# Both FFNs' normalisations on ScalarE, a sixth C product on GpSimd, and a new order of stages, in a fused macaron layer

## The chip, the cores and the metric

One core of one Trainium2 chip. The metric is the device time of one launch in microseconds (us), here the median of three runs.

## The reference

32 sequences of 256 tokens with H = 128 channels, float32. Three parts follow one another on the residual x:

```python
x = x + 0.5 * _L0_ffn_ref(_layernorm(x), Wg, bg, W1, b1, W2, b2)
x = x + _L0_attn_ref(_layernorm(x), norm_w, in_proj_w, conv_w, conv_b, ..., out_proj_w)
x = x + 0.5 * _L0_ffn_ref(_layernorm(x), Wg, bg, W1, b1, W2, b2)
```

The FFN has eight experts of 128 x 128 and takes, for each token, the output of the expert with the largest gate:

```python
logits = xf @ Wg + bg
idx = argmax(softmax(logits))
h = gelu(einsum('th,ehi->tei', xf, W1) + b1)       # exact gelu
y = einsum('tei,eih->teh', h, W2) + b2
out = y[idx]
```

The middle part is a Mamba block with its own residual (D_IN = 256, N = 16 states, convolution of 4 taps):

```python
xn = rmsnorm(x) * norm_w
x_path, z_path = split(xn @ in_proj_w.T)
x_path = silu(causal_conv(x_path) + conv_b)
dt_x, Bm, Cm = split(x_path @ x_proj_w.T)
dt = softplus(dt_x @ dt_proj_w.T + dt_proj_b)
h = exp(dt * A) * h + (dt * x_path) * Bm           # over the 256 tokens
y = sum_n(h * Cm) + D_param * x_path
return (y * silu(z_path)) @ out_proj_w.T + residual
```

## The kernel before

The 8192 tokens are cut into 16 chunks of 512 (two sequences). A software pipeline runs over iterations `i0` from -4 to 16. In one iteration the state recurrence of chunk i0 is made, the first FFN (f1) of chunk i0+3 and its second products for i0+2, the projections x, z, bc, dt of the Mamba block for i0+2 and i0+1, the out projection and the gate of the second FFN (f2) for i0-1, and the products of f2 for i0-1 to i0-3. Every iteration has 16 slots. Nothing schedules by itself: a `Plan` gives for each engine the slot (with .5 or a sub-position 0 to 3) at which a stage stands in that engine's program, and semaphores hold an instruction back until its inputs and its buffer are ready.

What the engines do in a slot s of the recurrence (half a head, one group q of four states, 1024 columns in two halves of 512, "units" 2s and 2s+1):

- GpSimd (`state_bx`, L1112) writes dtx * B into `hb`, two slots ahead.
- ScalarE (`make_decay`, L775) writes exp(A dt) of a half into one of three PSUM banks `dA`, two halves ahead. It waits until the half that last had this bank is read.
- VectorE (`state_unit`, L914) runs the recurrence of a half as a scan and then multiplies by C: scan in L926 and product in L930. For the slots in `POOL_C` (1, 2, 5, 9, 14) the scan writes to `hb` (L924), and GpSimd makes the product of both halves (`product_c`, L1120).
- TensorE (`sum_states`, L606) adds up the states of two slots into the PSUM bank `Y`.

Around it stand the other stages. Two PSUM banks `G` are shared by the transposes, gates and projections, in the order of the plan (`BANK` gives the bank, `g_full` and `g_free` the hand-over). A first product of an expert (`first_product`, L562 with the bias and L563) goes to the bank `PH`; ScalarE copies it out (`take_first`, L731), and the gelu over four experts comes later (`gelus`, L751), between two table loads. Second products (L594) of an FFN gather in the bank `PY`, which VectorE adds to X (L983). A layer norm has its statistics on VectorE (`norm_stats`), the inverse root on GpSimd (`inverse_root`, L1052) and the normalisation (`normalize`, L1079): (x - mean) * rstd, four instructions of 128 columns (L1085). The transposes of the result on TensorE (L542) go to a G bank, which ScalarE copies out (L724), the gate product (L661) and VectorE's one-hot code (L957 to L968) with its transposes (L670) follow.

The out projection (L641) of the plan's stage "out" writes bank 0 of G, after z0 in the same bank has been read by ScalarE's silu (L805). VectorE adds it to X (L983, the second such). The silu of x (L780) is made behind that of z, and needed by the products bc and dt (L550). ScalarE reads the bank of dt twice (L818, L820), then makes the softplus (L824, L826), GpSimd adds (L1140) and multiplies (L1145), and the results go through DRAM to be replicated. All DMAs are issued by SyncE in the order of its own plan.

## Time and profile before

| | us |
|---|---|
| median of 3 runs | 1329.93 |
| lowest and highest | 1327.08, 1342.4 |
| the profiled execution, its own time | 1330.48 |
| its span in the profile | 1328.7 |

The profile shows one execution. Engines are PE (TensorE), PEld (its weight loads), DVE (VectorE), ACT (ScalarE), POOL (GpSimd) and SP (SyncE). An idle time in brackets is that of the engine just before the instruction, and behind the arrow stands what released it. The granted clock is given as a share of 2.4 GHz. Line numbers are those of the kernel before.

### The profile page before, as it was taken

How to read it: one execution, taken by the hardware profiler on the slowest of the kernel's cores; microseconds unless marked ns; L12 is line 12 of the kernel's file. 1: busy time of each engine (PE TensorE's matmuls, PEld its weight loads, DVE VectorE, ACT ScalarE, POOL GpSimd, SP SyncE). 2: the span in 40 equal slices, each digit the busy share in tenths (PEclk: the TensorE clock that was granted, in tenths of full speed). 3: DMA queues.
4: the chain of work that ended last, by engine and by line, in shares of the span. 5: the costliest groups of instructions: out<-in, count | busy, mean ns of one | idle time of the engine just before them, and what ended most of it. 6: DMA issues, size and time to landing. Idle time of an engine off the chain costs nothing.

```text
span 1328.7 us, 16290 instructions
## 1 busy us (share of the span) xinstructions
PE 1142.2 (86%) x5188; PEld 579.9 (44%) x5188; DVE 1060.7 (80%) x1713; ACT 857.7 (65%) x1159; POOL 1067.7 (80%) x900
## 2 busy tenths in 40 slices
PE   6886868799999898999989898998989896969588
PEld 3432324244535444544445454454435443524246
DVE  2317989988898988888988988888888889888930
ACT  2327475777768687767768677767768686574531
...
DMA packets 60405, 130.02 MB, mean 98 GB/s; under 512 B 7744, under 2 KB 26864, under 8 KB 52128
## 3 DMA queue, kind: packets, MB, share of 16 engines
...
q8 instruction: 42, 0.69, 0.2%
...
## 4 chain that ended last, share of the span: by engine, by line
PE 59%; DVE 21%; ACT 8%; issue 6%; POOL 5%; SPq 0%; DMA 0%; DVEq 0%; ACTq 0%; POOLq 0%
PE PY L594 17%; PE PH L563 12%; PE G L550 9%; DVE dA L926 8%; PE Y L606 7%; DVE hb L924 4%; PE PH L562 4%; PE G L641 3%; DVE hb L930 3%; PE G L542 2%; PE dA L576 2%; POOL hb L1112 2%; DVE stat L905 2%; ACT hs L751 1%; ACT dA L775 1%
## 5 line engine op out<-in xcount | busy, mean ns | idle before, releaser
L1112 POOL TENSOR_TENSOR hb<-dtx_rep,bs 128x1024 f32<-128x1024 f32 x256 | 598.7, 2359 | 0.0
L926 DVE TENSOR_TENSOR_SCAN dA<-dA,hb 128x512 f32<-128x512 f32 x352 | 429.1, 1219 | 23.8 <-ACT dA L775 16.8
L775 ACT ACTIVATE dA<-dt_rep,A 128x512 f32<-128x512 f32 x512 | 343.7, 690 | 115.9 <-DVE hb L930 97.6
L594 PE MATMUL PY<-W,hs 128*128 128x128 f32 x2048 | 298.6, 289 | 0.0
L594 PEld LDWEIGHTS PY<-W,hs 128*128 128x128 f32 x2048 | 261.9, 196 | 82.8 <-issue 72.1
L731 ACT COPY hs<-PH 128x512 f32<-128x512 f32 x232 | 135.2, 583 | 237.7 <-PE PH L563 235.0
L563 PE MATMUL PH<-xnT,W 128*128 128x512 f32 x464 | 280.5, 688 | 0.0
L930 DVE TENSOR_TENSOR hb<-dA,cs 128x512 f32<-128x512 f32 x352 | 243.5, 692 | 24.8 <-DVE dA L926 0.5
L1120 POOL TENSOR_TENSOR hb<-hb,cs 128x1024 f32<-128x1024 f32 x80 | 188.7, 2359 | 85.0 <-DVE hb L924 85.0
L924 DVE TENSOR_TENSOR_SCAN hb<-dA,hb 128x512 f32<-128x512 f32 x160 | 186.4, 1206 | 8.9 <-ACT dA L775 6.8
L606 PE MATMUL Y<-hb,Sel 128*32 128x512 f32 x1024 | 161.3, 707 | 29.5 <-POOL hb L1120 19.6
L562 PE MATMUL PH<-ohT,Lm 24*128 24x512 bf16 x232 | 93.8, 404 | 44.9 <-ACT hs L731 42.8
L751 ACT ACTIVATE hs<-hs 128x2048 f32<-128x2048 f32 x58 | 110.5, 1912 | 0.3
L563 PEld LDWEIGHTS PH<-xnT,W 128*128 128x128 f32 x464 | 72.7, 197 | 57.0 <-issue 57.0
L943 DVE SCALAR_TENSOR_TENSOR xs<-G,Wc,xs 128x506 f32<-128x506 f32 (+2 forms) x96 | 67.5, 739 | 37.6 <-ACT xs L795 34.8
L562 PEld LDWEIGHTS PH<-ohT,Lm 24*128 24x128 bf16 x232 | 21.2, 91 | 146.7 <-ACT hs L731 82.6
L641 PE MATMUL G<-Wo,y 128*128 128x128 f32 x256 | 49.4, 373 | 32.3 <-ACT zs L805 32.3
L1057 POOL TENSOR_SCALAR neg<-mv 128x4 f32<-128x4 f32 x48 | 9.7, 201 | 81.9 <-DVE mv L911 81.9
L606 PEld LDWEIGHTS Y<-hb,Sel 128*32 128x32 f32 x1024 | 21.6, 115 | 109.6 <-issue 73.4
L1140 POOL TENSOR_TENSOR dt<-dt,sp 128x1024 f32<-128x1024 f32 x16 | 37.8, 2364 | 38.3 <-ACT sp L826 38.3
L641 PEld LDWEIGHTS G<-Wo,y 128*128 128x128 f32 x256 | 46.4, 280 | 45.2 <-issue 44.9
L957 DVE TENSOR_TENSOR G<-G,Bg 128x32 f32<-128x32 f32 x32 | 6.1, 190 | 73.4 <-PE G L661 73.4
...
## 6 DMA issues: line engine op xcount, KB each, us to landing
...
```

Of the source, the lines that this page charges most:

```text
L562: nc.tensor.matmul(PH[:, :], Lm[:, e, :], ohT[:, w, (it.i0 + off) % 2, :], start=True, stop=False)
L563: nc.tensor.matmul(PH[:, :], W1[:, e, :], xnT[:, w, :], start=False, stop=True).then_inc(ph_full, 1)
L594: last = nc.tensor.matmul(PY[:, P * j:P * (j + 1)], hs[:, w, e, P * j:P * (j + 1)], W2[:, e, :], start=False, stop=e == E - 1 and j == J - 1)
L606: last = nc.tensor.matmul(Y[D32 * g:D32 * (g + 1), :], Sel[:, :], hb[:, (2 * k + g // 2) % HR, g % 2], start=k == 0, stop=q == NQ - 1)
L641: last = nc.tensor.matmul(G[b][:, P * j:P * (j + 1)], y2[:, h, P * j:P * (j + 1)], Wo[:, h, :], start=h == 0, stop=h == HF - 1)
L731: nc.scalar.copy(hs[:, w, e, :], PH[:, :]).then_inc(ph_free, 1)
L775: nc.scalar.activation(dA[u % NA][:, :], dt_rep[:, h, g, :], ACT.Exp, scale=A[:, h, g, q:q + 1]).then_inc(decay, 1)
L924: nc.vector.tensor_tensor_scan(x_in_hb, a, x_in_hb, 0.0, ALU.mult, ALU.add).then_inc(scan, 1)
L926: nc.vector.tensor_tensor_scan(a, a, x_in_hb, 0.0, ALU.mult, ALU.add).then_inc(scan, 1)
L930: nc.vector.tensor_tensor(x_in_hb, a, cs[:, q, :], ALU.mult).then_inc(prod, 1)
L1112: nc.gpsimd.tensor_tensor(hb[:, s % HR], dtx_rep[:, h, 2 * m:2 * m + 2, :], bs[:, q, None, :].broadcast_to([P, 2, CH]), ALU.mult).then_inc ...
L1120: nc.gpsimd.tensor_tensor(hb[:, s % HR], hb[:, s % HR], cs[:, q, None, :].broadcast_to([P, 2, CH]), ALU.mult).then_inc(prod_p, 1)
```

## The change

Seven edits go together:

1. "out" no longer uses a G bank. It writes `Y`, the bank of the state sums, which is idle between two chunks, and stands one and a half slots earlier. The first sum of the next chunk waits until VectorE has read it (`out_read`).
2. Both `normalize` go from GpSimd to ScalarE, as four activations x * rstd + shift each, where GpSimd makes the new value shift = -mean * rstd (one small instruction more). f2's stands behind slot 7, f1's behind slot 14.
3. Slot 12 joins `POOL_C`: its product goes from VectorE to GpSimd.
4. Expert 4 of f1 in the steady iterations uses the bank `PY` instead of `PH`. It waits for VectorE's addition of f1 (`y_added`), and the second products of f2 wait for its copy.
5. First products of f1 (experts 4 to 7) and of all of f2 stand earlier, by up to a slot; the transposes oh_f1 stand in slot 5 instead of 6; on ScalarE dt0 comes half a slot later.
6. Decay 2 of the next chunk is made at the end of iteration slot 15 and decay 14 in slot 5, ahead of dt0 (`EARLY`); GpSimd makes the input of slot 5 right behind that of slot 4 (`EARLY_B`). ScalarE makes the silu of x ahead of that of z.
7. VectorE has new places between the two halves of a slot: f1's one-hot code at 1.25 instead of 1.0, the addition of "out" at 3.25 instead of behind that of f2 at 3.5.

The core of the diff:

```diff
-BANK = {"ln_f1": 0, "z0": 0, "out": 0, "bc": 0, ...
+BANK = {"ln_f1": 0, "z0": 0, "bc": 0, ..., "out": None}
 STEADY = Plan(
-    stages=[..., ("out", 3, 1), ("bc", 4, 1), ("dt1", 5, 0), ("dt0", 5, 1), ("oh_f1", 6, 0), ...
+    stages=[..., ("out", 2, 2), ("bc", 4, 1), ("dt1", 5, 0), ("dt0", 5, 1), ("oh_f1", 5, 1), ...
...
-    dve={"gate_f1": 1.0, "gated1": 1.5, "y_f2": [(3.5, -3)], "out": 3.5, ...
+    dve={"gate_f1": 1.25, "gated1": 1.5, "y_f2": [(3.5, -3)], "out": 3.25, ...
+IN_PY = (0, 4)
+EARLY = {(15, 0): 2, (5, 1): 14}
+EARLY_B = {2: 5}
-POOL_C = (1, 2, 5, 9, 14)
+POOL_C = (1, 2, 5, 9, 12, 14)
```

```diff
 def first_product(it, w, e, off):
-    it.wait_unit(pe, ph_free, w, e, 0)
-    nc.tensor.matmul(PH[:, :], Lm[:, e, :], ohT[...], start=True, stop=False)
-    nc.tensor.matmul(PH[:, :], W1[:, e, :], xnT[:, w, :], start=False, stop=True).then_inc(ph_full, 1)
+    if in_py(it.plan, w, e):
+        it.wait(pe, y_added[0], off - 1, 1, 1)
+        bank, full = PY, py_full
+    else:
+        it.wait_unit(pe, ph_free, w, e, 0)
+        bank, full = PH, ph_full
+    nc.tensor.matmul(bank[:, :], Lm[:, e, :], ohT[...], start=True, stop=False)
+    nc.tensor.matmul(bank[:, :], W1[:, e, :], xnT[:, w, :], start=False, stop=True).then_inc(full, 1)
 def sum_states(it, off, k):
     if k == 0:
-        it.wait(pe, gated, off, HF, 0)
+        it.wait(pe, out_read, off - 1, 1, 1)
 # "out" on TensorE
-    it.wait_free(pe, g_free, "out")
-            last = nc.tensor.matmul(G[b][:, P * j:P * (j + 1)], y2[...], Wo[:, h, :], ...)
-    last.then_inc(g_full[b], 1)
+            last = nc.tensor.matmul(Y[:, P * j:P * (j + 1)], y2[...], Wo[:, h, :], ...)
+    last.then_inc(out_made, 1)
 # ScalarE
+def normalize(it, w, off):
+    it.wait(act, rooted[w], off, 1, 1)
+    if it.has(off - 1):
+        Iteration(...).wait_read(act, g_free, f"ln_f{w + 1}")
+    for j in range(J):
+        last = nc.scalar.activation(xn[:, w, j, :], X[...], ACT.Identity,
+                                    scale=rstd[:, w, j:j + 1], bias=shift[:, w, j:j + 1])
+    last.then_inc(normed[w], 1)
 # ScalarE, the end of a slot
-    stages(it, s + 0.5)
+    for k in range(2):
+        if k:
+            stages(it, s + 0.5)
+        if (s, k) in EARLY and it.has(off):
+            make_decay(it, off, EARLY[s, k])
 # GpSimd, inverse_root for the two FFNs
+    nc.gpsimd.tensor_tensor(shift[:, w, :], neg[:, w, :], rstd[:, w, :], ALU.mult).then_inc(rooted[w], 1)
-def normalize(it, w, off):
-    ...
-        last = nc.gpsimd.tensor_scalar(xn[...], X[...], neg[...], rstd[...], ALU.add, ALU.mult)
```

In the rows below a name in brackets is the semaphore on which the instruction waits; "x3" in a row of its own stands for three of the kind above, without a wait.

TensorE around "out", before. L594 is the last second product of f2, L562 and L563 the first products, L606 a state sum, L641 "out":

```order
L594 MATMUL PY<-W,hs 128x128 [waits gelu_f2]
L594 MATMUL PY<-W,hs 128x128 x3
L562 MATMUL PH<-ohT,Lm 128x512 [waits ph_free]
L563 MATMUL PH<-xnT,W 128x512
L641 MATMUL G<-Wo,y 128x128 [waits g0_free,gated]
L641 MATMUL G<-Wo,y 128x128 x7
L606 MATMUL Y<-hb,Sel 32x512 [waits prod_p,prod,gated]
L606 MATMUL Y<-hb,Sel 32x512 x3
L562 MATMUL PH<-ohT,Lm 128x512 [waits ph_free]
L563 MATMUL PH<-xnT,W 128x512
```

The same place now (L617, L583 and L584, L629, L662):

```order
L583 MATMUL PH<-ohT,Lm 128x512 [waits ph_free]
L584 MATMUL PH<-xnT,W 128x512
L617 MATMUL PY<-W,hs 128x128 [waits gelu_f2]
L617 MATMUL PY<-W,hs 128x128 x3
L662 MATMUL Y<-Wo,y 128x128 [waits gated]
L662 MATMUL Y<-Wo,y 128x128 x7
L583 MATMUL PH<-ohT,Lm 128x512 [waits ph_free]
L584 MATMUL PH<-xnT,W 128x512
L629 MATMUL Y<-hb,Sel 32x512 [waits prod_p,prod,out_read]
L629 MATMUL Y<-hb,Sel 32x512 x3
```

"out" lost its wait for bank 0, and stands ahead of a first product instead of behind it. The first sum, which was behind "out" directly, now waits for VectorE to read it.

TensorE around the products bc and dt (L550), before, from the second half of dt on. The transposes oh_f1 are L670:

```order
L606 MATMUL Y<-hb,Sel 32x512 [waits prod_p,prod]
L606 MATMUL Y<-hb,Sel 32x512 x3
L592 MATMUL PY<-b_part,ohT 128x128 [waits gelu_f1,y_added_f2]
L594 MATMUL PY<-W,hs 128x128
L592 MATMUL PY<-b_part,ohT 128x128
L594 MATMUL PY<-W,hs 128x128
L592 MATMUL PY<-b_part,ohT 128x128
L594 MATMUL PY<-W,hs 128x128
L592 MATMUL PY<-b_part,ohT 128x128
L594 MATMUL PY<-W,hs 128x128
L670 MATMUL G<-Idb,oh 24x128 [waits g1_free,gate_f1]
L670 MATMUL G<-Idb,oh 24x128 x3
```

Now (L566 for the projections, L691 for oh_f1):

```order
L583 MATMUL PH<-ohT,Lm 128x512 [waits ph_free]
L584 MATMUL PH<-xnT,W 128x512
L566 MATMUL G<-xs,Wxdt 128x512 [waits g1_free]
L566 MATMUL G<-xs,Wxdt 128x512
L566 MATMUL G<-xs,Wxdt 128x512 [waits g0_free]
L566 MATMUL G<-xs,Wxdt 128x512
L691 MATMUL G<-Idb,oh 24x128 [waits g1_free,gate_f1]
L691 MATMUL G<-Idb,oh 24x128 x3
L629 MATMUL Y<-hb,Sel 32x512 [waits prod_p,prod]
L629 MATMUL Y<-hb,Sel 32x512 x3
```

oh_f1 moved from behind the sum and the first second product to directly behind dt0. It waits for bank 1, which dt1 had.

ScalarE between the taps of the convolution (L795) and the decays of the next chunk, before. L731 are copies of PH, L775 decays:

```order
L795 ACTIVATE xs<-G,Bc,Wc 128x512 [waits g1_full,summed]
L795 ACTIVATE xs<-G,Bc,Wc 128x512 [waits g0_full]
L731 COPY hs<-PH 128x512 [waits ph_full,w2_done_f1]
L775 ACTIVATE dA<-dt_rep,A 128x512 [waits prod]
L775 ACTIVATE dA<-dt_rep,A 128x512 [waits scan]
L731 COPY hs<-PH 128x512 [waits ph_full,w2_done_f2] x2
L775 ACTIVATE dA<-dt_rep,A 128x512 [waits prod,dt0_in]
```

Now (L836 taps, L766 copies, L812 decays, L753 the normalisations of f1):

```order
L836 ACTIVATE xs<-G,Bc,Wc 128x512 [waits g1_full,summed]
L836 ACTIVATE xs<-G,Bc,Wc 128x512 [waits g0_full]
L766 COPY hs<-PH 128x512 [waits ph_full,w2_done_f2]
L812 ACTIVATE dA<-dt_rep,A 128x512 [waits prod]
L812 ACTIVATE dA<-dt_rep,A 128x512 [waits scan]
L753 ACTIVATE xn<-X,shift,rstd 128x128 [waits g0_free,rooted_f1]
L753 ACTIVATE xn<-X,shift,rstd 128x128 x3
L766 COPY hs<-PH 128x512 [waits ph_full,w2_done_f2]
L812 ACTIVATE dA<-dt_rep,A 128x512 [waits prod,dt0_in]
```

The four normalisations stand between the decays of slot 15 and a copy of PH; the copies are those of one expert later.

## Rows read from the trace of the kernel before

**Rows 1.** Page of the profile, part 1: busy us, share of the span, instructions

```profile
PE 1142.2 (86%) x5188; PEld 579.9 (44%) x5188; DVE 1060.7 (80%) x1713; ACT 857.7 (65%) x1159; POOL 1067.7 (80%) x900
```

**Rows 2.** Chain of work that ended last: start us, us, what

```profile
412.54 3.44 PE G L641 x16
...
1013.04 3.56 PE G L641 x16
```

**Rows 3.** Timeline of TensorE, 700 to 790 us: start us, us, instruction, [idle before <-releaser]

```profile
712.74 3.53 PE L641 MATMUL G<-Wo,y 128*128 128x128 f32 x16 [2.14 <-ACT zs L805]
...
723.59 1.88 PE L550 MATMUL G<-xs,Wxdt 128*128 128x512 f32 x4
...
749.10 0.39 PE L562 MATMUL PH<-ohT,Lm 24*128 24x512 bf16 x1 [2.73 <-ACT hs L731]
...
755.94 0.66 PE L542 MATMUL G<-Id,xr 128*128 128x128 f32 x4 [1.23 <-POOL xr L1095]
...
761.71 1.98 PE L550 MATMUL G<-xrT,Win 128*128 128x512 f32 x4 [0.45 <-ACT xrT L724]
...
777.49 0.95 PE L661 MATMUL G<-Wg,xnT 128*128 128x8 f32 x8
...
786.93 3.17 PE L641 MATMUL G<-Wo,y 128*128 128x128 f32 x16 [2.14 <-ACT zs L805]
```

**Rows 4.** Timeline of VectorE, 700 to 790 us and after 1095

```profile
718.37 1.20 DVE L926 TENSOR_TENSOR_SCAN dA<-dA,hb 128x512 f32<-128x512 f32 x1
...
742.00 0.69 DVE L983 SCALAR_TENSOR_TENSOR X<-PY,X 128x512 f32<-128x512 f32 x1 [1.09 <-PE PY L594]
...
780.10 2.34 DVE L924 TENSOR_TENSOR_SCAN hb<-dA,hb 128x512 f32<-128x512 f32 x2 [0.21 <-DVE oh L968]
...
1173.62 1.23 DVE L926 TENSOR_TENSOR_SCAN dA<-dA,hb 128x512 f32<-128x512 f32 x1 [1.86 <-ACT dA L775]
```

**Rows 5.** Windows: busy us of PE, PEld, DVE, ACT, POOL; granted clock; DMA share; GB/s

```profile
262.00:265.00 3.00, 1.24 (x11) 1.17 (x11) 2.90 (x4) 2.99 (x4) 3.00 (x2) 1.00 0.00 0
712.00:715.00 3.00, 2.27 (x11) 2.30 (x11) 2.86 (x5) 2.98 (x4) 3.00 (x2) 0.58 0.00 0
826.00:829.00 3.00, 2.67 (x11) 0.95 (x6) 2.93 (x12) 2.23 (x4) 3.00 (x4) 0.50 0.01 3
```

**Rows 6.** Timeline of TensorE in three other stretches

```profile
263.86 2.02 PE L641 MATMUL G<-Wo,y 128*128 128x128 f32 x16 [1.76 <-ACT zs L805]
...
837.76 1.88 PE L550 MATMUL G<-xrT,Win 128*128 128x512 f32 x4
...
1291.49 0.26 PE L592 MATMUL PY<-b_part,ohT 24*128 24x128 bf16 x1 [0.85 <-ACT hs L751]
```

**Rows 7.** Groups of 562.5 to 862.5 us: count, busy us, mean ns, idle before

```profile
L926 DVE TENSOR_TENSOR_SCAN dA<-dA,hb 128x512 f32<-128x512 f32 x88 | 107.3, 1219 | 4.4 <-ACT dA L775 2.3 <-DVE oh L968 1.2 <-DVE xs L943 0.9
...
L563 PE MATMUL PH<-xnT,W 128*128 128x512 f32 x128 | 76.6, 681 | 0.0
...
L930 DVE TENSOR_TENSOR hb<-dA,cs 128x512 f32<-128x512 f32 x89 | 61.6, 692 | 6.2
L1120 POOL TENSOR_TENSOR hb<-hb,cs 128x1024 f32<-128x1024 f32 x20 | 47.2, 2359 | 15.4 <-DVE hb L924 15.4
...
L751 ACT ACTIVATE hs<-hs 128x2048 f32<-128x2048 f32 x16 | 30.6, 1914 | 0.1
...
L1085 POOL TENSOR_SCALAR xn<-X,neg,rstd 128x128 f32<-128x128 f32 x32 | 14.0, 452 | 0.8
...
L795 ACT ACTIVATE xs<-G,Bc,Wc 128x512 f32<-128x512 f32 x8 | 6.2, 778 | 7.8 <-PE G L550 7.7
...
L780 ACT ACTIVATE xs<-xs 128x1024 f32<-128x1024 f32 x4 | 4.2, 1058 | 0.0
```

**Rows 8.** Timeline of ScalarE, 700 to 790 us

```profile
724.59 0.68 ACT L820 ACTIVATE sp<-G,Bdt 128x512 f32<-128x512 f32 x1
...
777.66 1.28 ACT L757 ACT_TABLE_LOAD   x1
```

More of the change, by code:

```diff
@@ L46 @@
 LN_OFF = {0: 3, 1: -1}
-BANK = {"ln_f1": 0, "z0": 0, "out": 0, "bc": 0, "dt0": 0, "gate_f2": 0, "ln_p": 0, "x0": 0,
-        "gate_f1": 1, "z1": 1, "dt1": 1, "oh_f1": 1, "ln_f2": 1, "oh_f2": 1, "x1": 1}
+BANK = {"ln_f1": 0, "z0": 0, "bc": 0, "dt0": 0, "gate_f2": 0, "ln_p": 0, "x0": 0,
+        "gate_f1": 1, "z1": 1, "dt1": 1, "oh_f1": 1, "ln_f2": 1, "oh_f2": 1, "x1": 1, "out": None}
 OFF = {"ln_f1": 3, "gate_f1": 3, "oh_f1": 3, "ln_p": 2, "x1": 2, "x0": 2, "z0": 1, "z1": 1, "bc": 1, "dt1": 1, "dt0": 1,
@@ L183, in g_uses, with in_py, count @@
     return n + sum(BANK[use] == BANK[name] and has(i, OFF[use]) for use in seq[:seq.index(name)])
+def in_py(plan, w, e):
+    return plan is STEADY and (w, e) == IN_PY
 def w1_uses(i, w, e):
-    n = sum(has(k, off) for k in range(FIRST, i) for *_, off in plan_of(k).w1_order)
+    def count(k, order):
+        return sum(has(k, off) and not in_py(plan_of(k), v, u) for *_, v, u, off in order)
     order = plan_of(i).w1_order
     at = [unit[2:4] for unit in order].index((w, e))
-    return n + sum(has(i, off) for *_, off in order[:at])
+    return sum(count(k, plan_of(k).w1_order) for k in range(FIRST, i)) + count(i, order[:at])
 def direct_no(w, chunk, e):
@@ L747, in gelus @@
                     it.wait_unit(act, ph_free, w, E - 1, 1)
+                    if w == 0 and it.plan is STEADY:
+                        it.wait(act, py_free, 0, 1, 1)
                 for k in range(2):
@@ L787, in stages @@
                         copy_out(it, f"ln_f{w + 1}", xnT[:, w, :])
+                if t == at.get("norm_f2") and it.has(-1):
+                    normalize(it, 1, -1)
+                if t == at.get("norm_f1") and it.has(4):
+                    normalize(it, 0, 4)
                 if t == at.get("ln_p") and it.has(2):
@@ L848, in body @@
                     take_units(it, s, 0)
-                    if it.has(off):
+                    if it.has(off) and 2 * t not in EARLY.values():
                         make_decay(it, off, 2 * t)
@@ L1020, in stages @@
                 if t == at.get("stats_f2") and it.has(-1):
[L1021 removed]
+                    it.wait(dve, out_read, -1, 1, 1)
                     norm_stats(it, 1, -1)
@@ L1127, in stages @@
                     inverse_root(it, 1, -1)
-                if t == at.get("norm_f2") and it.has(-1):
-                    normalize(it, 1, -1)
                 if t == at.get("root_p") and it.has(2):
```

94 lines of the change are left out of this document (47 added, 47 removed).

## The prediction

> **What bounds the kernel now.** I read the shares of the engines first, then the groups of a stretch of four periods, the chain, the timelines of each engine over one period, and last the granted clock. No engine is full: TensorE 86%, VectorE and GpSimd 80%, ScalarE 65% of the span [rows 1]. So the time is set by a loop of waits. In the chain the out projection returns every 75.06 us on average (1013.04 - 412.54 over eight periods) [rows 2]. Periods come in two kinds. I lay a short one out between three marks [rows 3, 4]: VectorE adds the first FFN to X at 742.00; 19.7 us later TensorE starts the x products (761.71); and 54.5 us after those (25.2 to the out projection at 786.93, then, by the period before, 29.3 from 712.74 to 742.00) comes the next addition, right behind the last second product. That is 74.2 us.
>
> In it TensorE waits four times, 6.6 us in all [rows 3]: 2.14 before the out projection, until ScalarE has read z0 out of the bank that "out" needs; 2.73 before a first product, because the copy of PH stands behind a table load and the first gelu; and two short ones. The wait before "out" costs more than itself. Its granted clock is 0.58 in 712 to 715 [rows 5], the level of 1.2 GHz for most of it, and the sixteen passes of "out" take 3.53 us there, where the same sixteen took 2.02 us at 263.86, with the clock at 1.00 [rows 5, 6]. I count 1.5 us for such a fall. In the long kind of period the fall behind the gelu lasts longer (0.50 at 826 to 829) [rows 5], and the x products start 21.5 us after the addition (837.76, the addition being at 786.93 + 29.3) instead of 19.7 [rows 3, 6].
>
> **First addition to x products: 0 to -0.4 us.** The product of slot 12 leaves VectorE: two instructions of 0.69 us; a slot with them takes 3.8 us, one without 2.3, so 1.5 [rows 4, 7]. They lie between the addition and the decay that holds up xrT, so xrT is ready earlier; only the 0.45 us wait before the x products can go. Expert 4 of the first FFN now goes to PY and fills the 2.73 us wait with 1.4 us of product and a sum. But the next unit still waits for a copy behind the second gelu, and the transposes of xr still hang on VectorE's statistics and GpSimd's root and normalisation, and come 14 us after the addition (755.94, behind 1.23 us of wait for GpSimd) [rows 3, 4]: that chain is untouched. The wait moves behind it. I take 0, and the same mixture of short and long.
>
> **X products to VectorE's second recurrence of slot 1: -0.5 us.** Before, gate_f1 ends 16.7 us after the x products (777.49 + 0.95) and the second recurrence of slot 1 starts at +19.5 (half of the pair at 780.10) [rows 3, 4]. Now one first-product unit less lies in between (64 units cost 76.6 us in their L563 part, so 1.2, and about 1.4 with L562) [rows 7]. Against that, ScalarE has four normalisations to do between the decays of slot 15 and the copy for which TensorE's next unit waits. No row shows such an instruction. By size, two SBUF rows (L780, 1058 ns for 1024 elements, and L751, 1914 for 2048) give 0.83 ns an element; from the 778 ns of L795, which also has scale and bias as operands, 384 elements fewer leave 0.46 us, and four overlapping ones some 1.5 us. Bounds: 1.2 us below, four times 778 ns, 3.1 us, above [rows 7]. (The Trainium skill, page "ScalarE: Activation LUTs", section on the cost of an ACTIVATE, gives 186 ns + 0.833 ns per element + 93 ns per pointer operand, 93 ns of it overlapped: 1.64 us for four, which would add 0.1 us a period.) With 1.5 us the copy ends 7.55 us after the x products, where TensorE wanted it at 6.7: a wait of 0.8 us. gate_f1 then ends at 16.3. But ScalarE is later too: its second table load, which ended at 778.94 (+17.2) [rows 8], ends at +18.3, and the decay of the second half at +19.0. Since the first recurrence now stands ahead of the gating, VectorE goes on at +19.0 instead of +19.5.
>
> **To the second addition: -1.4 us with the half above.** VectorE from +19.0: rest of slot 1 and y2 1.7, slot 2 2.25, half of slot 3 1.9, X+out 0.7, other half 1.9, X+PY 0.6, statistics 1.3: slot 4 starts at +29.4, before at +30.85 (718.37 is 5.63 behind its "out") [rows 4]. VectorE's wait for "out" and TensorE's 2.14 are gone. Slot 4 takes 3.8, the first recurrence of slot 5 1.2: +34.4. Behind that ScalarE makes one decay (0.7) and reads dt1 twice (1.25, the second in 0.68 [rows 8]): +36.35. TensorE is faster: from gate_f1's end at 16.3 through z, two units, two w2, "out" at full clock (2.0), a unit, the sum, bc, a unit, dt1 and dt0 I count 18.1 us, so +34.4. And here is the new wait. The transposes oh_f1 now stand directly behind dt0 and need the bank of dt1, which ScalarE lets go at +36.35. Before they came behind a sum and 2.3 us of second products. Queued behind them are the sum of slots 2 and 3 and everything of the first FFN. From there 16.6 us of TensorE work lead to the second addition, as before (725.4 to 742.0) [rows 3, 4]: +53.0 instead of +54.5. Of TensorE's 3.6 us at "out", 1.95 come back as this wait. VectorE, done with slot 9 before, idles.
>
> **The clock takes part of it: +0.9 us.** A wait of 1.95 us is near to the 2.14 us after which the clock fell. Bounds: 0 and 1.5 us; I take a fall in six of ten periods. The Trainium skill speaks against this term: its page "TensorE: Matmul & The Clock Gate", section "Part 1: The HAM clock gate", has the ramp at under 1% of a typical kernel span and advises against fitting it. Here 1.5 us of 75 are 2% for each fall. By that rule both the old 1.5 and the new 0.9 drop out, nothing is left of the gain in a period, and the sum would be 1322; the measured passes decide, so I keep the term.
>
> **Other edits: nothing.** The GpSimd balance is two normalisations (2 x 1.75 with overlap) out, one product of 2.36 and two small ones of 0.27 in [rows 7]; the sixth product ends about 5.2 us behind the x products, 0.5 before its sum is wanted. The early recurrence input, C2 right behind C1 and x_silu first move work inside ScalarE's and GpSimd's idle time. norm_f2 fits where ScalarE waited for PH. SP's c2 now waits for the GpSimd product, some 0.6 us later, with more than 20 us in hand.
>
> **Ends: -8 us.** The last four chunks have no first FFN ahead of them or little; VectorE is nearly full. There the 1.5 us count in full, four times: -6.0. The decay pulled ahead of dt0 takes away a wait of VectorE in slot 7, 1.86 us at 1173.62 [rows 4] and some 1.7 in the period before: -3.5. At the very end ScalarE normalises behind both gelus. Before, the transposes ran during them, and second products began at 1291.49, 0.85 behind [rows 6]; now 1.5 us of normalisation, the transposes and their latency come on top, 3.8, less one unit and copy of 2.2 that was done earlier: +1.6.
>
> **Sum.** A period: 0 - 1.4 + 0.9 - 0.1 (short waits) = -0.6. Twelve periods: -7. With the ends -15. The profiled execution took 1330.48 us by its own clock (span 1328.7), so 1315.5; the median of three is 0.55 lower: 1315.
>
> **Rivals.** First, the clock does not fall at oh_f1, and with fuller stretches the long kind of period vanishes too: -1.5 and the 0.9 between a short period and the mean, twelve times, and -8 at the ends: 1293. For it: the wait of 1.76 us before "out" at 263.86 left the clock full [rows 5, 6]. Against it: the second gap behind the gelu stays. 0.30.
>
> Second, the fall comes in each period: -1.4 + 1.5 a period comes to +1 in twelve, with the ends 1323, no change that can be told. 0.20.
>
> Third, slower: ScalarE's normalisations cost what L795 costs. The chain from the x products through ScalarE's gelus grows by 1.6 us a period, and TensorE's wait for PH reaches 2.4 us, long enough for a fall as well as that at oh_f1. -1.4 + 1.5 + 1.6 = +1.7, times twelve, less 8: 1342. It decides from about 2.6 us for the four. For it: copies and decays queue behind them. Against it: the sizes. 0.12. My forecast has 0.38.
>
> **Range.** The main case with its bounds goes from 1305 to 1326; the rivals stretch it to 1291 and 1338. A measurement of this kernel can tell about 1% from no change, 13 us. Faster by over 1% (below 1316.6): rival one and half of the main case, 0.50. Slower: 0.12. Same: 0.38.
>
> **What would show it.** Right: "out" without a wait and at full clock; a wait of about 2 us at oh_f1 on ScalarE's read of dt1; VectorE waiting 1 to 3 us for the second products before the addition; four normalisations in 1.5 us; VectorE's wait at slot 7 gone; a mean period near 74.4. Wrong: no wait at oh_f1 (the gain is then 2 us and more), normalisations of 0.6 us and longer, or a new wait of VectorE for bx or of TensorE for the GpSimd product of slot 12.

## The result

| | us |
|---|---|
| predicted | 1315.0 (1291 to 1338) |
| changed kernel, median of 4 runs | 1356.07 (1347.27 to 1359.36) |
| kernel before, measured beside it, median of 4 | 1328.51 |
| ratio, 95% interval | 1.0157 (1.0110 to 1.0204) |
| profiled execution of the changed kernel, its own time and span | 1354.01, 1352.2 |

The change made the kernel 1.6% slower, outside the range and on the other side. (The ratios here and below leave aside an execution that took over 1.5% longer than the fastest one of its kernel.) Read in the two traces, the 23.5 us between the spans (1328.7 and 1352.2) lie like this:

| stretch, by its first x product | before | changed | difference |
|---|---|---|---|
| start to the first x product after 300 us | 311.63 | 326.92 | +15.3 |
| ten periods from there | 749.80 | 764.64 | +14.8 |
| from there to the end | 267.3 | 260.6 | -6.6 |

The ends came out near the forecast of -8. The ten periods went from a mean of 74.98 to 76.46 us, where 74.4 was forecast, and the start had no term in the sum at all.

The page of the changed kernel, part 1 and the row of the granted clock in forty slices, against [rows 1]:

```profile
PE 1150.1 (85%) x5188; PEld 572.5 (42%) x5188; DVE 1036.9 (77%) x1681; ACT 899.5 (67%) x1287; POOL 1055.0 (78%) x820
...
PEclk9888969897989999898979989797999988878689
```

VectorE and GpSimd have less to do than before, ScalarE 42 us more. TensorE, with the same 5188 instructions, is busy 8 us longer: its instructions take longer, there are not more of them.

**The fill.** ScalarE's timeline over the first 30 us. The first fence is the changed kernel, the second the kernel before; the number in brackets is the idle time ahead:

```profile
25.41 1.65 ACT L753 ACTIVATE xn<-X,shift,rstd 128x128 f32<-128x128 f32 x4 [14.89 <-POOL shift L1108]
27.07 1.28 ACT L777 ACT_TABLE_LOAD   x1
28.36 0.60 ACT L777 ACTIVATE hs<-PH 128x512 f32<-128x512 f32 x1
```

```profile
10.34 1.28 ACT L742 ACT_TABLE_LOAD   x1
17.70 0.60 ACT L742 ACTIVATE hs<-PH 128x512 f32<-128x512 f32 x1 [6.08 <-PE PH L576]
```

ScalarE works in order. In the fill's plan the normalisation of chunk 1 stands ahead of the direct gelus of chunk 0, and its data come late; so it waits 14.89 us, and the first gelu starts at 28.36 instead of 17.70. On GpSimd nothing was queued behind that wait.

**A steady period.** TensorE's timeline of the changed kernel from an addition of f1 (VectorE's row, 761.54) to the x products (L566, 784.52) and on to oh_f1 (L691), against [rows 3, 4]:

```profile
761.54 0.69 DVE L1025 SCALAR_TENSOR_TENSOR X<-PY,X 128x512 f32<-128x512 f32 x1 [1.26 <-PE PY L617]
```

```profile
768.64 0.38 PE L583 MATMUL PH<-ohT,Lm 24*128 24x512 bf16 x1 [0.36 <-ACT hs L766]
768.96 1.13 PE L584 MATMUL PH<-xnT,W 128*128 128x512 f32 x2
770.01 0.39 PE L691 MATMUL G<-Idb,oh 128*24 128x128 bf16 x4
772.84 0.60 PE L583 MATMUL PH<-ohT,Lm 24*128 24x512 bf16 x1 [2.43 <-ACT hs L766]
773.37 2.07 PE L584 MATMUL PH<-xnT,W 128*128 128x512 f32 x2
775.45 1.11 PE L558 MATMUL G<-Id,xr 128*128 128x128 f32 x4
...
784.52 3.62 PE L566 MATMUL G<-xrT,Win 128*128 128x512 f32 x4
...
809.76 1.95 PE L662 MATMUL Y<-Wo,y 128*128 128x128 f32 x16
...
819.79 1.98 PE L566 MATMUL G<-xs,Wxdt 128*128 128x512 f32 x4 [0.92 <-ACT bcT L745]
823.55 0.38 PE L691 MATMUL G<-Idb,oh 128*24 128x128 bf16 x4 [1.78 <-ACT sp L858]
```

Much is as forecast. "Out" (L662) has no wait and takes 1.95 us instead of 3.17 to 3.56 [rows 2, 3]. The new wait at oh_f1 stands where it was put, on the softplus's read of the dt1 bank, with 1.78 us for 1.95. But between the addition and the x products, where the forecast had 0 to -0.4 us, there are 23.0 us, and every pass behind the wait of 2.43 us takes double: L584 has 2.07 us for what took 1.13 just ahead. The windows of the changed kernel show why (busy us of PE, PEld, DVE, ACT, POOL; granted clock; DMA share; GB/s):

```profile
769.00:772.00 3.00, 1.41 (x7) 0.47 (x6) 2.86 (x4) 2.98 (x3) 2.68 (x8) 1.00 0.01 3
772.00:775.00 3.00, 2.16 (x3) 0.60 (x3) 2.97 (x12) 1.98 (x4) 3.00 (x5) 0.57 0.00 0
775.00:778.00 3.00, 3.00 (x7) 1.31 (x7) 2.70 (x4) 1.79 (x3) 2.90 (x6) 0.50 0.46 175
...
784.00:787.00 3.00, 3.00 (x5) 1.53 (x6) 0.00 (x0) 0.47 (x1) 3.00 (x2) 0.50 0.25 87
787.00:790.00 3.00, 3.00 (x6) 0.80 (x5) 1.76 (x3) 1.08 (x2) 3.00 (x2) 0.59 0.77 213
790.00:793.00 3.00, 3.00 (x20) 1.39 (x18) 2.48 (x4) 2.76 (x6) 3.00 (x3) 1.00 0.57 229
...
820.00:823.00 3.00, 1.77 (x4) 0.47 (x3) 3.00 (x4) 2.16 (x4) 1.75 (x2) 1.00 0.09 22
823.00:826.00 3.00, 2.45 (x19) 1.24 (x19) 2.86 (x4) 2.97 (x5) 2.12 (x1) 1.00 0.02 5
```

The clock falls to the level of 1.2 GHz behind that gap and stays there for some 17 us, though TensorE is busy all through, and the x products still run in it (3.62 us for the 1.88 to 1.98 of [rows 3, 6]). At the wait of oh_f1 (820 to 826) it does not fall at all. In the kernel before, the low stretch behind the gelu was some 3.5 us in one period and 10 in the next, here in its windows:

```profile
750.00:753.00 3.00, 3.00 (x14) 0.70 (x12) 2.86 (x4) 2.97 (x4) 2.84 (x6) 0.50 0.01 3
753.00:756.00 3.00, 1.77 (x6) 0.46 (x5) 2.86 (x12) 2.13 (x4) 2.90 (x6) 0.93 0.08 29
...
825.00:828.00 3.00, 2.67 (x14) 0.97 (x7) 2.97 (x7) 2.97 (x5) 2.92 (x5) 0.52 0.01 3
...
834.00:837.00 3.00, 3.00 (x16) 1.02 (x11) 2.95 (x4) 2.27 (x4) 2.82 (x7) 0.77 0.00 0
```

In the changed kernel it is 7 to 17 us in each period (read in windows of 0.5 us). VectorE and ScalarE then wait for the x products. The fence shows two groups of the changed kernel over 590 to 890 us, four periods; the last numbers are the idle time before them. In the kernel before the same two groups waited 2.0 us (taps on VectorE) and 7.8 us (L795) in such a stretch:

```profile
L985 DVE SCALAR_TENSOR_TENSOR xs<-G,Wc,xs 128x506 f32<-128x506 f32 (+2 forms) x24 | 17.1, 742 | 19.3 <-ACT xs L836 18.7
...
L836 ACT ACTIVATE xs<-G,Bc,Wc 128x512 f32<-128x512 f32 x8 | 6.2, 777 | 20.9 <-PE G L566 20.9
```

So addition to x products went from a mean of 20.5 to 22.4 us, and x products to addition from 54.5 to 54.05. The second was forecast as 53.0 (without the clock term): it is 52.9 in four of ten periods, and 53.8 to 55.4 in the other six, in which the x products themselves ran wholly or partly at the low clock.

### The profile page after: what moved, and what is told of

It is laid out like the page before. It is cut to its first block, busy times and chain, and to the rows that moved or that the text cites. A ratio compares the mean times of both kernels' runs of the same rounds, so it can differ in the third digit from the quotient of the medians.

```text
span 1352.2 us, 16303 instructions
## 1 busy us (share of the span) xinstructions
PE 1150.1 (85%) x5188; PEld 572.5 (42%) x5188; DVE 1036.9 (77%) x1681; ACT 899.5 (67%) x1287; POOL 1055.0 (78%) x820
## 4 chain that ended last, share of the span: by engine, by line
PE 45%; ACT 19%; DVE 19%; issue 11%; POOL 4%; SPq 1%; DMA 0%; DVEq 0%; ACTq 0%; POOLq 0%
PE PY L617 15%; PE PH L584 10%; DVE dA L968 8%; ACT hs L788 5%; PE Y L629 5%; ACT dA L812 4%; PE G L566 4%; DVE hb L966 3%; PE PH L583 3%; DVE hb L972 3%; ACT hs L766 2%; ACT L794 2%; PE G L558 2%; PE PY L615 2%; DVE X L1025 2%
## 5 line engine op out<-in xcount | busy, mean ns | idle before, releaser
L968 DVE TENSOR_TENSOR_SCAN dA<-dA,hb 128x512 f32<-128x512 f32 x320 | 390.3, 1220 | 15.3 <-ACT dA L812 9.0
L812 ACT ACTIVATE dA<-dt_rep,A 128x512 f32<-128x512 f32 x512 | 339.5, 688 | 66.7 <-DVE hb L972 49.7
L617 PE MATMUL PY<-W,hs 128*128 128x128 f32 x2048 | 303.6, 293 | 0.0
L617 PEld LDWEIGHTS PY<-W,hs 128*128 128x128 f32 x2048 | 266.6, 199 | 85.7 <-issue 74.9
L1153 POOL TENSOR_TENSOR hb<-hb,cs 128x1024 f32<-128x1024 f32 x96 | 226.3, 2358 | 88.4 <-DVE hb L966 88.4
L766 ACT COPY hs<-PH 128x512 f32<-128x512 f32 x219 | 127.6, 583 | 232.5 <-PE PH L584 204.1
L584 PE MATMUL PH<-xnT,W 128*128 128x512 f32 x438 | 274.5, 711 | 0.0
L966 DVE TENSOR_TENSOR_SCAN hb<-dA,hb 128x512 f32<-128x512 f32 x192 | 224.6, 1205 | 27.1 <-ACT dA L812 24.9
L972 DVE TENSOR_TENSOR hb<-dA,cs 128x512 f32<-128x512 f32 x320 | 221.2, 691 | 22.6 <-DVE dA L968 0.5
L629 PE MATMUL Y<-hb,Sel 128*32 128x512 f32 x1024 | 156.3, 684 | 30.3 <-POOL hb L1153 22.8
L583 PE MATMUL PH<-ohT,Lm 24*128 24x512 bf16 x219 | 91.5, 418 | 50.2 <-ACT hs L766 48.1
L584 PEld LDWEIGHTS PH<-xnT,W 128*128 128x128 f32 x438 | 71.8, 206 | 56.7 <-issue 56.7
L583 PEld LDWEIGHTS PH<-ohT,Lm 24*128 24x128 bf16 x219 | 20.1, 92 | 151.7 <-ACT hs L766 109.0
L566 PE MATMUL G<-xs,Wxdt 128*128 128x512 f32 x128 | 62.6, 615 | 13.1 <-ACT bcT L745 13.1
L629 PEld LDWEIGHTS Y<-hb,Sel 128*32 128x32 f32 x1024 | 21.8, 113 | 111.1 <-issue 55.8
L753 ACT ACTIVATE xn<-X,shift,rstd 128x128 f32<-128x128 f32 x128 | 52.4, 481 | 20.7 <-POOL shift L1108 20.7
```

The costliest lines, as they stand in the source:

```text
L583: nc.tensor.matmul(bank[:, :], Lm[:, e, :], ohT[:, w, (it.i0 + off) % 2, :], start=True, stop=False)
L584: nc.tensor.matmul(bank[:, :], W1[:, e, :], xnT[:, w, :], start=False, stop=True).then_inc(full, 1)
L617: last = nc.tensor.matmul(PY[:, P * j:P * (j + 1)], hs[:, w, e, P * j:P * (j + 1)], W2[:, e, :], start=False, stop=e == E - 1 and j == J - 1)
L629: last = nc.tensor.matmul(Y[D32 * g:D32 * (g + 1), :], Sel[:, :], hb[:, (2 * k + g // 2) % HR, g % 2], start=k == 0, stop=q == NQ - 1)
L766: nc.scalar.copy(hs[:, w, e, :], PH[:, :]).then_inc(ph_free, 1)
L812: nc.scalar.activation(dA[u % NA][:, :], dt_rep[:, h, g, :], ACT.Exp, scale=A[:, h, g, q:q + 1]).then_inc(decay, 1)
```

## The experiments

For each trace I add up the windows of 1.5 us between 300 and 1125 us in which the granted clock is under 0.75 ("low"), and take the mean of ten periods from the first x product after 300 us. "y to x" is the time from the addition of f1 to the x products in most of these periods. The executions of one kernel scatter by about 1% around their median, so a difference of a few us between medians is none. The kernel before was measured again beside each group of runs, with medians from 1327 to 1335 us; the ratios are to those, and they are the safer comparison between groups (e1 to e4; e5 to e8; e9 to e12; e13 to e16). Periods, low time and "y to x" are each read from one traced execution.

| kernel | median us (runs) | ratio to before, 95% | period | low | y to x |
|---|---|---|---|---|---|
| before | 1328.51 (4) | | 74.98 | 111 | 19.7 / 21.4 |
| changed | 1356.07 (4) | 1.0157 (1.0110-1.0204) | 76.46 | 138 | 21.7 to 23.0 |
| e1 fill order | 1344.0 (4) | 1.0103 (1.0032-1.0175) | 75.74 | 132 | 21.6 to 23.0 |
| e2 first products of before | 1340.35 (10) | 1.0036 (0.9993-1.0078) | 73.59 | 65 | 19.1 / 21.3 |
| e3 norms on GpSimd | 1327.58 (10) | 0.9962 (0.9928-0.9996) | 75.05 | 134 | 22.0 / 23.0 |
| e4 slot 12 on VectorE | 1356.36 (4) | 1.0172 (1.0094-1.0250) | 76.16 | 143 | 21.7 to 23.0 |
| e5 filler in the gap (on e1) | 1308.98 (4) | 0.9852 (0.9799-0.9905) | 73.22 | 47 | 19.08 |
| e6 = e2 + norms on GpSimd | 1333.84 (10) | 1.0071 (1.0030-1.0112) | 75.16 | 77 | 19.1 |
| e7 = e2 + fill order | 1331.02 (10) | 1.0028 (0.9989-1.0067) | 73.91 | 81 | 19.08 |
| e8 before + "out" in Y | 1341.01 (10) | 1.0093 (1.0064-1.0123) | 75.88 | 116 | 19.7 / 21.5 |
| e9 before + filler | 1338.84 (10) | 1.0079 (1.0054-1.0104) | 75.20 | 81 | 20.7 |
| e10 filler of one product | 1345.49 (4) | 1.0101 (1.0043-1.0159) | 75.85 | 108 | 21.7 to 23.0 |
| e11 f1's rows of before | 1341.40 (10) | 1.0078 (1.0037-1.0119) | 75.41 | 68 | 19.1 / 21.4 |
| e12 f2's rows of before | 1334.89 (10) | 1.0041 (1.0010-1.0071) | 75.17 | 126 | 21.6 / 23.0 |
| e13 filler elsewhere | 1352.11 (4) | 1.0132 (1.0038-1.0226) | 75.32 | 48 | 19.60 |
| e14 = e5 + norms on GpSimd | 1308.91 (4) | 0.9842 (0.9785-0.9898) | 73.76 | 45 | 19.1 |
| e15 changed + filler | 1316.30 (10) | 0.9919 (0.9873-0.9965) | 72.56 | 32 | 19.05 |
| e16 = e5 + slot 12 on VectorE | 1322.01 (10) | 0.9918 (0.9883-0.9953) | 73.69 | 38 | 19.72 |

### The fill: e1

```diff
 FILL[-3]
-    act={"ln_f1": 0, "norm_f1": 1}
+    act={"ln_f1": 0, "norm_f1": 9.5}
```

> The changed kernel, with one number changed: in the fill (iteration -3) ScalarE makes f1's normalisation of chunk 1 at slot 9.5, behind the eight direct gelus of chunk 0, instead of at slot 1 ahead of them. Theory F (the fill): in the changed kernel this normalisation waits 14.9 us for data ahead of the gelus, and that alone moved the first x products from 95.25 to 105.9 us. Then the first x products come back to about 96 and the time is 1356 - 10 = 1346 us. Rival: the delay has another cause or is absorbed before the first steady period (the transposes of chunk 1 now come late): first x products stay at 103 or later, time 1353 to 1358.

1344.0 us, 12 less than the changed kernel (ratio 1.0103 for 1.0157). The first x products start at 94.45, and those of the first period after 300 us at 313.0 instead of 326.9. ScalarE's timeline of e1: the first gelu is back at 17.83, and the four normalisations take the same time without a wait.

```profile
17.83 0.60 ACT L777 ACTIVATE hs<-PH 128x512 f32<-128x512 f32 x1 [6.09 <-PE PH L597]
...
34.97 1.64 ACT L753 ACTIVATE xn<-X,shift,rstd 128x128 f32<-128x128 f32 x4
```

Theory F holds. One number in the plan was some 12 of the 28 us between the medians.

### Undoing one edit: e2, e3, e4

e2 takes the rows of first products and copies from the kernel before and sets `IN_PY = None`, with the two waits for `py_free` out. e3 gives GpSimd both `normalize` at their old places. e4 is one number:

```diff
-POOL_C = (1, 2, 5, 9, 12, 14)
+POOL_C = (1, 2, 5, 9, 14)
```

> The changed kernel, with the places of all first products and of their copies as before, and expert 4 of f1 in PH instead of PY (edits 4 and 5 undone except for oh_f1 and dt0; all else as changed). Theory W (the steady periods grew from 74.98 to 76.46 us because the new places leave a wait of 2.4 us behind the second gelu of f2, after which TensorE's clock stays at its low level up to the x products): the clock is back up before the x products, these start about 20 us after the addition of f1 instead of 22 to 23, and twelve periods give 12 x 1.5 = 18 us: 1338 us. Rival N (ScalarE's normalisations or its other extra work lengthen the period): the period stays near 76.4, time 1352 to 1358.

> The changed kernel, with all normalisations of both FFNs back on GpSimd at their places of before (edit 2 undone, all else as changed). Theories F and W together: the fill is as before (first x products near 96), the steady periods stay near 76.4: 1346 us. Rival N (the normalisations on ScalarE are what lengthens the periods): fill and periods both come back, 1356 - 10 - 18 = 1328 us or less. Against both: GpSimd, with six products and the normalisations, becomes the bound: over 1350.

> The changed kernel, with the product of slot 12 back on VectorE (edit 3 undone, all else as changed). Theories F and W: the period keeps its length to 0.5 us, since neither the gap behind the gelu nor the clock hangs on it, and the ends lose 1.5 us in each of some four chunks: 1356 to 1364 us. Rival P (the sixth product holds up GpSimd's inputs and so VectorE, or TensorE's sum): periods near 75, 1338 to 1345 us.

e2 came to 1340.35: theory W, with periods of 73.59 (expected about 75) and half the low time. Ten such periods are 29 us shorter than in the changed kernel and the time is only 16 us less: in the traced execution the start took 6.7 us longer (333.7 to the first x products after 300 us) and the last stretch 8.0 us (268.7 instead of 260.6), where the first products of before come back too. But e3 came to 1327.58, as rival N had it, 16 us under e1, and kept both its low time (134) and its long way to the x products (22 to 23 us). So W and N each seemed to explain the whole of the steady loss. Part of e3 can be read: x products to "out" take 22.1 us in its shorter periods and 22.9 in those of e1, since the wait of 0.71 us for the copy behind the normalisations (0.8 in the prediction) is gone. The periods of the two profiled executions differ by 0.7 us (75.74 and 75.05), 8 of the 16 us. The other 8 are in no trace: the profiled execution of e1 (1335.77) is the fastest of its four and lies 8.2 us under their median, that of e3 (1327.71) lies at its own. e4 changed nothing, as W expected.

### The clock itself: e5, and its control e13

Both add work that nothing uses to the kernel of e1. It has the same three products into an idle G bank in each steady iteration; e5 puts them ahead of the gap, e13 in slot 9, where TensorE runs without a wait.

```diff
+FILLER = (11, 3)
+if s == FILLER[0] and it.plan is STEADY and it.has(3) and it.has(-1):
+    it.wait_read(pe, g_free, "ln_f2")
+    for _ in range(FILLER[1]):
+        nc.tensor.matmul(G[1][:, :], Win[:, 0:P], W1[:, 0:4, :].rearrange("p e t -> p (e t)"), start=True, stop=True)
```

> The kernel of e1_fill_order (1344.0 us), with work added that nothing uses: in slot 11 of each steady iteration TensorE makes three products of 128 x 512 (about 1.9 us) into bank 1 of G, which is idle there, directly ahead of the first product for which it waits 2.43 us behind the second gelu of f2. Theory C (it is the low clock behind this gap, not the place of the products, that costs the steady periods): the wait shrinks to about 0.5, the clock stays up, the x products start about 20 us after the addition of f1 instead of 21.6 to 23, the periods of 78 us vanish: mean 74.3 instead of 76.2, time 1344 - 12 x 1.8 = 1322 us. Rival D (the gap's delay by itself and the ScalarE work set the period, and the clock is a by-product): added work can't help, 1342 to 1350 us.

> Control of e5_filler: the same three unused products of 128 x 512, but in slot 9, where TensorE runs without a wait of 0.3 us or more, and not in the gap behind the gelu of f2. Theory C (the gain of e5_filler came from filling that gap): here the products cost what they take, 2.84 us in each of 12 periods, and the low clock behind the gelu stays: 1344 + 34 = 1378 us (1360 to 1385). Rival (any added work of TensorE keeps its clock up, wherever it stands): 1305 to 1330 us.

e5: 1308.98 us, 35 less than e1 (by the ratios, 0.9852 for 1.0103, 33) and below the kernel before by 1.5% (0.9799 to 0.9905). TensorE's timeline in e5, and its windows:

```profile
748.44 2.84 PE L730 MATMUL G<-W,Win 128*128 128x512 f32 x6
...
753.39 0.39 PE L584 MATMUL PH<-ohT,Lm 24*128 24x512 bf16 x1 [0.41 <-ACT hs L772]
753.70 1.12 PE L585 MATMUL PH<-xnT,W 128*128 128x512 f32 x2
755.69 0.66 PE L559 MATMUL G<-Id,xr 128*128 128x128 f32 x4 [0.86 <-POOL xr L1134]
...
760.85 1.88 PE L567 MATMUL G<-xrT,Win 128*128 128x512 f32 x4
```

```profile
751.00:754.00 3.00, 2.59 (x10) 0.99 (x10) 2.93 (x11) 2.65 (x5) 2.92 (x5) 1.00 0.01 3
...
757.00:760.00 3.00, 3.00 (x18) 1.07 (x16) 2.86 (x4) 2.19 (x4) 3.00 (x5) 1.00 0.17 57
```

With 2.84 us of idle work the wait of 2.43 shrinks to 0.41, the clock stays at 2.4 GHz, and the x products come 19.08 us after the addition. Eight of the ten periods lack any fall there. In the last five of them the period is 71.99 us, 3 us under that of the kernel before. That is the change and the added products together, against a kernel whose clock still falls; what the change alone is worth with the clock up on both sides, no run shows.

e13 was to cost 34 us and cost 8 by the medians (1352.11, from 1338.93 to 1362.7); without the execution of 1362.7, as in the ratio, the median is 1345.37, and nothing is left that can be told from scatter. Its rows show the same gap, but a short fall:

```profile
773.61 0.38 PE L584 MATMUL PH<-ohT,Lm 24*128 24x512 bf16 x1 [2.43 <-ACT hs L772]
```

```profile
772.00:775.00 3.00, 1.39 (x3) 0.53 (x3) 2.93 (x12) 2.75 (x4) 3.00 (x4) 0.84 0.01 3
775.00:778.00 3.00, 2.70 (x8) 1.11 (x7) 3.00 (x4) 1.79 (x3) 2.90 (x7) 0.59 0.56 153
778.00:781.00 3.00, 3.00 (x17) 1.02 (x15) 2.86 (x4) 2.13 (x4) 2.92 (x5) 1.00 0.08 27
```

The x products follow at 781.91, 19.60 us after the addition. In the first period after 300 us the same kernel has the same gap, but a fall of 17 us, and its x products come 22.99 us after the addition (which is at 306.13):

```profile
317.43 0.60 PE L584 MATMUL PH<-ohT,Lm 24*128 24x512 bf16 x1 [2.43 <-ACT hs L772]
...
329.12 3.62 PE L567 MATMUL G<-xrT,Win 128*128 128x512 f32 x4
```

```profile
318.00:321.00 3.00, 2.99 (x7) 1.17 (x6) 2.97 (x9) 1.45 (x3) 2.90 (x8) 0.50 0.33 79
...
330.00:333.00 3.00, 3.00 (x5) 0.75 (x3) 0.74 (x1) 1.00 (x2) 3.00 (x3) 0.50 0.48 113
```

So with one program and one length of gap the long fall costs 3.4 us, and the gap with its short fall 0.5 (19.60 against the 19.08 of e5): the low clock is the cost, as theory C has it. The periods of e13 without a long fall are 75.1 us, 3.1 above the 71.99 of e5: 2.6 between x products and addition (55.5 for 52.9), where the added products stand, and 0.5 between addition and x products. The low time is 48 us, as in e5. So the rival is partly right too: work put elsewhere shortened the fall, though not the gap, and what that gave back about paid for the work. Each fall here stands behind a wait; how long the low level then lasts hangs on something else as well, which no run here isolates.

### How much filler, and on which kernel: e10, e9, e15

e10 is e5 with `FILLER = (11, 1)`. e9 puts the three products into the kernel before, at the start of slot 11. e15 puts them into the changed kernel, with its fill as it is.

> The kernel of e5_filler with one unused product of 0.95 us instead of three (2.84 us). TensorE's wait behind the gelu is then about 1.5 us instead of 2.43 (without) or 0.41 (with three). Theory: what counts is how much of the stretch TensorE idles, so the clock falls in some periods and for shorter: time between 1344 (none) and 1309 (three), about 1325 us. Rival (any wait of this place drops the clock, the three products helped since they closed it): as without, 1338 to 1346 us. Second rival (a wait of 1.5 us is as harmless as that of 1.78 us at oh_f1): 1305 to 1312 us.

> The kernel before, with the same unused work as in e5_filler: in slot 11 of each steady iteration TensorE makes three products of 128 x 512 (0.95 us each) ahead of the first product that waits 2.73 us behind the second gelu of f2. Theory C (in this kernel, too, it is the low clock behind that gap that costs, 3 us in one period and 9 in the next): no low clock there, the x products 19.1 to 19.7 us after each addition of f1, periods of 75.0 - 1.4 = 73.6 us, time 1330 - 17 = 1313 us (1306 to 1320). Rival (the kernel before has balanced this gap: the wait for GpSimd's xr behind it stays, so that the added work only takes its place): 1325 to 1333 us.

> The changed kernel with the three unused products in slot 11 and nothing else, the fill as changed. Two costs that add up: 1356.1 - 35 (gap behind the gelu) = 1321 us, with periods of 72 and first x products near 106. Rival (the later start shifts periods and clock against each other, so that falls stay in most periods): over 1330 us.

e10: 1345.49, as without; one product leaves a wait of 1.81 us, then one of 1.18 for xr, and the clock falls in each period. e9: my expectation was wrong, 1338.84 instead of 1313. TensorE's timeline of e9:

```profile
764.53 0.39 PE L563 MATMUL PH<-ohT,Lm 24*128 24x512 bf16 x1 [1.07 <-ACT hs L737]
...
767.66 0.66 PE L543 MATMUL G<-Id,xr 128*128 128x128 f32 x4 [1.69 <-POOL xr L1101]
...
768.56 2.08 PE L564 MATMUL PH<-xnT,W 128*128 128x512 f32 x2
...
774.45 1.88 PE L551 MATMUL G<-xrT,Win 128*128 128x512 f32 x4
```

The gap of 2.73 us is closed, but in its place stand a wait for the next copy (1.07) and one for xr (1.69), close together, and behind them the clock falls (L564 at 2.08). The added products only took the place of waits, and the time rose although the low time fell from 111 to 81 us: the sum of low time by itself is not the price, it counts what then ends last. e15: 1316.3, 40 under the changed kernel, the two costs adding up as expected (1321). It beats the kernel before by 0.8% (0.9873 to 0.9965), and all but two of its ten periods are 71.97 us. With the same filler the fill's order is then worth 1316.3 - 1309.0 = 7 us by the medians, for 12 without it.

### The parts with less low clock: e14, e16

> The kernel of e5_filler with both FFNs' normalisations on GpSimd as before. Sizes the normalisations on ScalarE while the clock is held up. My figure of the prediction: a wait of 0.8 us at a copy, so x to out 22.1 instead of 22.87 and periods of 71.2 instead of 71.98: 1309 - 9 = 1300 us. Rival (GpSimd, with six products and the normalisations, now ends last in some waits, as in e6_w1_before_norms_gpsimd): periods of 72.5 or more, 1315 us or more. Second rival (what made e3_norms_gpsimd 16 us faster than e1_fill_order was only the clock's pattern): 1307 to 1311 us.

> The kernel of e5_filler with the product of slot 12 back on VectorE (edit 3 undone). In the steady periods my prediction gave this edit 0 to 0.4 us, since the chain from the addition over the statistics to xr is untouched, and 1.5 us in each of the last four chunks: 1309 + 6 = 1315 us. Rival (with the clock up VectorE is what ends last between the addition and the x products): 1.5 us a period more, 1309 + 24 = 1333 us. Second rival (nothing, as e4_slot12_dve against the changed kernel): 1307 to 1311 us.

e14: 1308.91, equal to e5, and its fill has GpSimd's normalisation as e3's. So once the gap is filled it makes no difference to the time which engine normalises: the 0.71 us at the copy are gone, but the state sum of TensorE waits 1.51 us for GpSimd's product instead, as in e6, where GpSimd has six products and the normalisations:

```profile
763.31 1.63 PE L630 MATMUL Y<-hb,Sel 128*32 128x512 f32 x8 [1.51 <-POOL hb L1156]
```

The second rival had the right time, 1307 to 1311 us, but its reason (the clock's pattern alone) isn't shown: one wait was exchanged for another. e16: 1322.01, 13 us over e5. The x products have a wait of 0.5 us again and come at 19.72 instead of 19.08; undisturbed periods are 72.73 instead of 71.99. The sixth product brings 0.7 us a period, half of the 1.5 that VectorE is spared.

### Putting parts together: e6, e7, e11, e12

e6 is e2 with the normalisations on GpSimd, e7 is e2 with the fill of e1. e11 and e12 split edit 5 on the kernel of e1: e11 has f1's rows (and expert 4) of before, e12 f2's.

> The changed kernel with the first products, PY and both FFNs' normalisations as before (edits 2, 4 and most of 5 undone, so that edits 1, 3, 6, 7 and oh_f1, dt0 stay). Theory of independent costs (fill 11 us; new places of first products 1.5 us a period through the clock; normalisations on ScalarE 0.8 us a period through the copy that they hold up, as x to out was 22.09 in e3_norms_gpsimd and 22.86 in e1_fill_order): periods of 73.4 - 0.8 = 72.6 us, time 1340 - 11 - 10 = 1319 us. Rival: each of the two edits alone already frees the period, and VectorE is the bound then: periods of 73.4 as in e2_w1_of_before, 1329 us.

> The kernel of e2_w1_of_before (1340 us) with the fill's normalisation behind the direct gelus, as in e1_fill_order. Additive: 1340 - 11 = 1329 us, first x products near 95, periods unchanged at 73.4. Rival: the earlier start only shifts the clock's pattern against the periods, and these get longer: 1335 to 1345 us.

> The kernel of e1_fill_order (1344.0 us) with f1's first products and their copies at the places of before and expert 4 in PH, f2's as changed. Theory: it is f1's rows with expert 4 in PY that bring TensorE to the copy behind the second gelu with nothing left to wait for at xr, so the gap leads into a fall in each period; with f1's rows of before it is as e7_w1_before_fill: 1331 us, periods of 74. Rival (it is f2's rows, which crowd the stretch from 14 on): 1340 to 1346 us.

> The kernel of e1_fill_order (1344.0 us) with f2's first products and their copies at the places of before, f1's and expert 4 in PY as changed. The counterpart of e11_f1_rows_before. Theory (f1's rows are the cause): 1340 to 1346 us, falls of 9 to 17 us behind the gelu in each period. Rival (f2's rows): 1331 us.

e7 came to 1331.02, as the additive theory had it. e6 came to 1333.84, not 1319: neither theory, since its sums wait up to 1.50 us for GpSimd. e12 went against its theory: 1334.89, nearer to the rival's 1331 and below e1 with nearly the same low time (126), as x products to "out" take 21.0 to 22.7 us. e11 (1341.40, not 1331) has little low time (68), yet its x products to "out" take 25.1 us: f1's last unit now stands behind the x products together with all of f2's, and TensorE meets three waits on copies there (0.82, 0.71, 0.39). In this pair of runs the rows of f1 decide how long the clock is low, those of f2 how crowded the stretch behind the x products is. The two tables belong together.

### "Out" alone: e8

The kernel before with edit 1 and the place 3.25 on VectorE.

> The kernel before, with edit 1 alone: the out projection goes to the bank Y, one and a half slots earlier, and VectorE adds it at 3.25. My step on this edit: its wait of 2.14 us and the low clock behind it (1.5 us) go, and as oh_f1 stays behind the sum, no wait takes their place except one of VectorE: -1.4 to -2.0 us a period, 12 to 15 periods: 1331 - 20 = 1311 us (1305 to 1318). Rival (the earlier place gains nothing, as the wait was covered by work of ScalarE and VectorE that ends last): 1327 to 1334 us.

1341.01, 0.9% slower instead of 1.4% faster. TensorE's timeline of e8 around the first sum (L608) behind "out":

```profile
791.81 1.06 PE L608 MATMUL Y<-hb,Sel 128*32 128x512 f32 x8 [1.26 <-DVE X L983]
794.15 0.39 PE L564 MATMUL PH<-ohT,Lm 24*128 24x512 bf16 x1 [1.27 <-ACT hs L731]
```

"Out" starts 21.5 us after the x products instead of 25, but the addition of f1 comes no earlier (53.3 to 56.3 us after them, mostly 54.8 and more, instead of 54.5). The wait of 2.14 us is replaced by two of 1.26 and 1.27, because the first sum must now wait until VectorE has read `Y`. In the changed kernel the first products moved earlier cover this.

## Why the prediction was wrong

**The step that failed most** is "First addition to x products: 0 to -0.4 us", with its "I take 0, and the same mixture of short and long". It measured +1.9 us a period (20.5 to 22.4). The step followed the waits rightly, even to "the next unit still waits for a copy behind the second gelu", and the wait shrank from 2.73 to 2.43 and 0.36. What it took as given was the clock behind the wait. In the short periods of the kernel before, TensorE reached the transposes of xr early and idled there for 1.23 us, so a short fall cost little. Expert 4 in PY and the earlier first products changed that: e11, with f1's rows of before, has the waits of 2.73 and 1.21 us again and its x products 19.1 or 21.4 us after the addition. With passes at double length for 7 to 17 us TensorE became what ends last up to the x products. e5 shows the size: with the clock up, the same stretch takes 19.08 us.

**"Other edits: nothing"** failed in the fill. The prediction said that norm_f2 fits into ScalarE's waits and looked at no normalisation ahead of the steady periods. The start cost 11.9 us up to the transposes of chunk 1 (36.57 against 48.47), and e1 gave back 12. The rule that would have caught it stands in the case itself: name what is queued behind a new wait.

**"The clock takes part of it: +0.9 us"** put the fall in the wrong place. The wait at oh_f1 was there (1.78 for 1.95), and the clock stayed at 1.00 there: each of the periods from 300 us on has one low stretch, and it lies behind the gelu. The wait before "out" of 2.14 us had dropped it in the kernel before, so the step went by length alone. But e13 has low stretches of unlike length behind equal waits of 2.43 us (3.5 us, and 17 in its first period after 300 us), so the length of one wait does not decide.

The Trainium skill, page "TensorE: Matmul & The Clock Gate", section "Part 1: The HAM clock gate", has the ramp, the slow first stretch of a kernel's matmuls, at under 1% of a typical kernel span. That figure does not carry over to falls that come back in each period: here the clock is low for 138 of 825 us, and filling one gap was worth 35 us. The prediction set it aside and was right to, yet kept far too little for the clock.

**Right steps.** X products to the second addition: forecast 53.0 against 54.5, measured 52.9 wherever the low clock doesn't reach it; "out" without a wait and at full clock; no wait of VectorE left at slot 7. Four normalisations: 1.5 us forecast, 1.64 measured, 481 ns each. (The estimate of 1.64 us from the page "ScalarE: Activation LUTs" of the Trainium skill, section "What ACT_TABLE_LOAD costs", agrees with it.) The wait at the copy behind them: 0.8 forecast, 0.71 measured.

**Right in part by luck.** Ends: -8 forecast, -6.6 measured. Undoing slot 12 (e4) lengthened that stretch by 3.3 us, where the forecast had 6.0, and e1, with the same code there, already differs from the changed kernel by 2.9. Undoing the first products lengthened it by 8.0 (e2, against the changed kernel) and by 5.1 (e7, against e1), and for those the forecast had no term. Rival three had the direction and the period (+1.7 forecast, +1.5 measured) by a wrong mechanism: it wanted normalisations of 778 ns.

**Slips in the sum.** From 54.5 to 53.0 is 1.5 us, where the sum takes 1.4, and the 1342 of rival three lies above the 1338 at which the range ends. Neither changes the outcome.

**What stays open:** what sets how long the low level lasts behind a gap; and how much more than 8 us the normalisations on GpSimd gain in e3, since e1's traced execution is not a typical one of its four.
